# Relational layer with layer normalisation: first half in quarters, later turns and normalising, and the bias added to x by GpSimd

## What is computed

```python
# adj: (8, 1024, 1024) int32, x: (8, 1024, 128) float32
# relation ids are 1..4, weight: (4, 128, 128), bias: (128,)
masks = (adj[None] == rel_ids[:, None, None, None]).astype(x.dtype)
h = jnp.einsum('rbnm,bmd->rbnd', masks, x)
y = jnp.einsum('rbnd,rdo->bno', h, weight)
z = x + (y + bias)
out = (z - mean(z)) / sqrt(var(z) + 1e-5)      # over the last axis
```

## Time and profile before

| | us |
|---|---|
| median of 3 runs (126.42 to 127.32) | 127.29 |
| the profiled execution | 128.38 |
| its span | 126.6 |
| PE busy | 104.6 (83%) |
| DVE busy | 96.2 (76%) |
| ACT busy | 83.4 (66%) |
| POOL busy | 79.8 (63%) |

### The profile page before, as it was taken

The page is one execution under the profiler, slowest core; times in us unless marked ns, Lnnn a source line. Parts: engine busy times, 40 slices in busy tenths (PEclk is TensorE's granted clock), DMA queues, the critical chain, the costliest instruction groups (busy, mean ns, idle before and its releaser), DMA issues.

```text
span 126.6 us, 1876 instructions
## 1 busy us (share of the span) xinstructions
PE 104.6 (83%) x551; PEld 85.0 (67%) x559; DVE 96.2 (76%) x243; ACT 83.4 (66%) x114; POOL 79.8 (63%) x76
## 2 busy tenths in 40 slices
PE   5933399989999789899999999999999999997100
PEld 2312288687878567678887887788879886896000
DVE  0249925277949999999999999999999997639820
ACT  4056780766649178699589939994999499951400
POOL 6008000067253989899989989999999899043510
PEclk9996557999999999999999999999999999999855
DMA  4999999999999999999999999999999700400620
GB/s 116 409 422 430 425 422 432 422 430 405 434 419 419 427 417 425 410 436 417 422 365 409 425 422 359 421 427 427 388 281 418 311 18 0 166 0 0 250 87 8
DMA packets 7362, 42.15 MB, mean 333 GB/s; under 512 B 819, under 2 KB 1206, under 8 KB 3254
## 3 DMA queue, kind: packets, MB, share of 16 engines
q1 hardware_dynamic: 7350, 42.01, 81.7%
HBM read 37.82 MB, written 4.19 MB: 332 GB/s over the span
## 4 chain that ended last, share of the span: by engine, by line
DMA 25%; DVE 22%; PE 18%; ACT 11%; POOL 11%; issue 6%; SPq 2%; DVEq 0%; POOLq 0%; ACTq 0%
DMA adj_sb<-in_adj_dram 25%; PE h_ps L187 13%; POOL scale L217 10%; ACT maskT L355 9%; DVE mask L426 6%; DVE stats L205 4%; DVE var_eps L214 4%; DVE total L440 3%; PE tp_ps L178 2%; PE y_ps L199 2%; DVE mean_var L210 2%; DVE out_sb L221 2%; ACT out_sb L374 1%; ACT h_sb L362 1%; SPq L244 1%
## 5 line engine op out<-in xcount | busy, mean ns | idle before, releaser
L355 ACT ACTIVATE maskT<-tp_ps 128x2048 fp32r<-128x2048 fp8e5 x32 | 59.7, 1873 | 8.1 <-PE tp_ps L178 8.1
L426 DVE TENSOR_SCALAR mask<-adj_sb 128x2048 uint8<-128x2048 uint32 x32 | 39.7, 1266 | 16.2 <-DMA adj_sb<-in_adj_dram 16.1
L217 POOL TENSOR_TENSOR scale<-var_eps,power 128x4 f32<-128x4 f32 (+1 forms) x17 | 44.3, 2608 | 0.6 <-DVE var_eps L214 0.6
L187 PE MATMUL h_ps<-maskT,x_hi 128*128 128x512 f32 (+1 forms) x136 | 35.7, 406 | 1.1 <-ACT maskT L355 0.9
L187 PE MATMUL h_ps<-maskT,x_lo 128*128 128x512 f32 (+1 forms) x136 | 33.8, 391 | 0.0
L178 PEld LDWEIGHTS tp_ps<-identity,mask 128*128 128x128 f32 x128 | 20.3, 204 | 13.8 <-DVE mask L426 10.2
L187 PEld LDWEIGHTS h_ps<-maskT,x_hi 128*128 128x128 f32 x136 | 24.7, 197 | 6.6 <-ACT maskT L355 2.3
L178 PE MATMUL tp_ps<-identity,mask 128*128 128x128 f32 x128 | 22.3, 300 | 7.9 <-DVE mask L426 7.8
L374 ACT ACTIVATE out_sb<-total,shift,scale 128x128 f32<-128x128 f32 x31 | 13.7, 488 | 19.8 <-POOL shift L319 19.8
L187 PEld LDWEIGHTS h_ps<-maskT,x_lo 128*128 128x128 f32 x136 | 23.5, 189 | 3.9
L199 PE MATMUL y_ps<-w_sb,h_sb 128*128 128x128 f32 x128 | 17.3, 277 | 1.6 <-ACT h_sb L362 1.3
(11 more groups left out here) (32 smaller groups left out, 33.3 us busy)
## 6 DMA issues: line engine op xcount, KB each, us to landing
adj_sb<-in_adj_dram SPq DMA_DIRECT2D x32, 1024.0 KB, 12.2
x_sb<-in_x_dram SPq DMA_DIRECT2D x8, 512.0 KB, 5.9
out_dram<-out_sb SPq DMA_DIRECT2D x7, 512.0 KB, 16.5
out_dram<-out_sb SPq DMA_DIRECT2D x1, 256.0 KB, 2.4
out_dram<-out_sb SPq DMA_DIRECT2D x2, 128.0 KB, 1.9
w_sb<-in_L_gnn_weight_dram SPq DMA_DIRECT2D x1, 64.0 KB, 6.5
bias_rows<-in_L_gnn_bias_dram SPq DMA_DIRECT2D x3, 0.5 KB
```

Source lines behind the costliest of these rows:

```text
L187: last = nc.tensor.matmul(h_ps[:, bank, 0:n], (x_hi, x_lo)[part][:, slot, t, :], maskT[:, places, t // WORD, t % WORD, :], start=(first an ...
L217: nc.gpsimd.tensor_tensor(scale[:, slot, tiles], var_eps[:, slot, tiles], power[:, tiles], ALU.pow).then_inc(done, by)
L355: nc.scalar.activation(maskT[:, u % NMT], turned_codes(u % NTP), ACT.Copy, accum_out=counts[:, u:u + 1]).then_inc(expanded, 1)
L426: nc.vector.tensor_scalar(mask[:, u % NMASK], adj_sb[:, u % NADJ].bitcast(u32), CAP, SET, ALU.min, ALU.mult).then_inc(masked, 1)
```

## The change

It has five parts.

- **Bias.** The bias is loaded once, over all partitions, on ACT's queue, together with the weight. The bf16 split, its placing, and the spreading products on PE (one per half, two for the last) are gone. Instead POOL adds the bias to all of `x_sb` of a batch (`add_bias`), right behind the `lo` of that batch; DVE's `add` waits for it (`biased`). In the general path the same add stands too.
- **First half in quarters.** The products, the copy and the order of the first half go by units instead of by half. POOL, not ACT and DVE, makes the parts of batch 0. PE gets 8 and 4 products on a scratch tile in between (`keep_warm`).
- **Later turns.** In the loop PE issues the products with `x_hi` before the turn of the unit 2hf+3 instead of after it.
- **Later normalising on ACT.** ACT normalises half hf-3 in each round instead of half hf-2.
- **Check and last half.** The check for other relations is made before the last adds, and its product stands ahead of the last products. SP loads x of the next batch one place later in its order.

The core of the diff:

```diff
+        def add_bias(x_slot, done):
+            nc.gpsimd.tensor_tensor(x_sb[:, x_slot], x_sb[:, x_slot],
+                                    bias_rows[:, :].unsqueeze(1).to_broadcast([P, TILES, D]), ALU.add).then_inc(done, 1)
-        def spread_bias(y, tiles):
-            n = tiles.stop - tiles.start
-            nc.tensor.matmul(y[:, 0:n, :], spread[:, :], bias_parts[:, 0:n, :], start=True, stop=False)
...
@@ sync
-            load_unit(1)
-            sp.wait_ge(bias_cleared, 1)
-            for q in PARTS:
-                sp.dma_start(bias_rows[q:q + 1, :], bias.unsqueeze(0)).then_inc(bias_loaded, 16)
-            sp.dma_start(w_sb[:, 0, :], weight[0]).then_inc(weights_loaded, 16)
-            for u in range(2, UNITS):
+            for u in range(1, UNITS):
                 load_unit(u)
-                if u % CH == 1 and u // CH + 1 < B:
+                if u % CH == (2 if u >= CH else 3) and u // CH + 1 < B:
                     load_batch(u // CH + 1)
-                if u == 3:
-                    load_batch(1)
@@ gpsimd
+            def bias_in(b):
+                if b == 0:
+                    pool.wait_ge(bias_loaded, 16)
+                pool.wait_ge(lo_made, b + 1)
+                add_bias(b % NX, biased)
-            split_bias()
+            hi(0)
+            lo(0)
+            bias_in(0)
             for b in range(B):
                 if b + 1 < B:
                     hi(b + 1)
...
                 if b + 1 < B:
                     lo(b + 1)
+                    bias_in(b + 1)
                 scales_half(2 * b)
@@ scalar
+            copy_quarter(0, 0)
+            expand(2)
+            copy_quarter(0, 1)
+            expand(3)
+            for hf in range(1, HALVES - 1):
+                if hf >= 2:
                     copy_half(hf - 1)
                 expand(2 * hf + 2)
                 expand(2 * hf + 3)
-                if hf >= 2:
-                    finish_half(hf - 2)
+                if hf >= 3:
+                    finish_half(hf - 3)
             copy_half(HALVES - 2)
+            finish_half(HALVES - 4)
+            copy_quarter(HALVES - 1, 0)
             finish_half(HALVES - 3)
-            copy_quarter(HALVES - 1, 0)
             copy_quarter(HALVES - 1, 1)
@@ vector
             def add(b, y, tiles, count, by):
                 dve.wait_ge(projected, count)
+                dve.wait_ge(biased, b + 1)
...
+            find_others()
             add_half(HALVES - 2)
             measure_half(HALVES - 2)
             finish_half(HALVES - 3)
-            find_others()
@@ tensor
+            turn(0)
+            keep_warm(8)
+            hi_quarter(0, 0)
+            turn(1)
+            lo_quarter(0, 0)
+            turn(2)
+            hi_quarter(0, 1)
+            lo_quarter(0, 1)
+            turn(3)
...
+            for hf in range(2, HALVES - 1):
+                hi_products(hf)
                 if 2 * hf + 3 < UNITS:
                     turn(2 * hf + 3)
-                hi_products(hf)
-                if 2 * hf + 4 < UNITS:
-                    turn(2 * hf + 4)
-                if hf >= 1:
-                    project_half(hf - 1)
+                project_half(hf - 1)
                 lo_products(hf)
+                if 2 * hf + 4 < UNITS:
+                    turn(2 * hf + 4)
```

More of the change, by code:

```diff
@@ L131, in relational_layer @@
         g_split = sem("g_split")
+        g_biased = sem("g_biased")
         g_masked = sem("g_masked")
@@ L198, in project @@
                 for r in range(relations):
-                    last = nc.tensor.matmul(y[:, n, :], h_of(r)[:, s], w_sb[:, r, :], start=False,
-                                            stop=(r == relations - 1 and s == tiles.stop - 1))
+                    last = nc.tensor.matmul(y[:, n, :], h_of(r)[:, s], w_sb[:, r, :], start=(r == 0),
+                                            stop=(r == relations - 1))
             last.then_inc(done, by)
@@ L379, in finish_half @@
                 finish(hf // 2, range(HT * (hf % 2) + 1, HT * (hf % 2) + HT, O), 2 * (hf + 1), 2)
+            act.dma_start(bias_rows[:, :], bias.unsqueeze(0).to_broadcast([P, D])).then_inc(bias_loaded, 16)
+            act.dma_start(w_sb[:, 0, :], weight[0]).then_inc(weights_loaded, 16)
             expand(0)
-            act.wait_ge(topped, 1)
-            nc.scalar.activation(flat(x_hi[:, 0]), flat(x_top[:, :]).bitcast(fp32), ACT.Copy).then_inc(hi_made, 1)
             expand(1)
-            for hf in range(HALVES - 1):
-                if hf >= 1:
+            copy_quarter(0, 0)
[3 more added lines that the diff above has]
+            for hf in range(1, HALVES - 1):
+                if hf >= 2:
                     copy_half(hf - 1)
@@ L483, in find_others @@
                 nc.vector.tensor_scalar(above[:, 1:2], above[:, 0:1], FULL, None, ALU.is_gt).then_inc(flag_step, 1)
-            def place_bias():
-                dve.wait_ge(bias_split, 3)
-                for q, part in zip(PARTS, (bias_rows, bias_rest, bias_fine)):
-                    last = nc.vector.tensor_copy(bias_parts[q:q + 1], upper(part[q:q + 1, :]).unsqueeze(1).to_broadcast(
-                        [1, HT, D]))
-                last.then_inc(bias_split, 1)
             convert(0)
             top(0)
-            convert(1)
-            dve.wait_ge(topped, 1)
-            take_lo(nc.vector, 0, 0, lo_made)
-            convert(2)
-            place_bias()
-            convert(3)
+            for u in (1, 2, 3):
+                convert(u)
+            top(1)
             convert(4)
-            for hf in range(HALVES - 1):
-                for u in (2 * hf + 5, 2 * hf + 6):
+            convert(5)
+            for hf in range(1, HALVES - 1):
+                for u in (2 * hf + 4, 2 * hf + 5):
                     if u < UNITS:
@@ L514, in _ @@
             finish_half(HALVES - 3)
-            find_others()
+            dve.wait_ge(flag_counted, 1)
+            nc.vector.tensor_copy(flag[:, :], tp_ps[0:1, 0, 0:1]).then_inc(flag_ready, 1)
             add_quarter(0)
@@ L650, in _ @@
                     for half in range(2):
-                        spread_bias(y_ps[:, half], HALF[0])
                         project(lambda r: h_all[:, r], y_ps[:, half], R, HALF[half], g_projected, 1)
```

70 lines of the change are left out of this document (29 added, 41 removed).

## The result

| | before | after |
|---|---|---|
| median, us (lowest to highest) | 127.31 (126.42 to 127.34) | 133.71 (132.76 to 134.26) |
| profiled execution, its span | 128.38, 126.6 | 133.56, 131.8 |

The changed kernel takes 1.051 times as long, interval 1.044 to 1.059: +6.4 us, where 132.7 us in all was forecast.

What follows compares the result with a forecast made beforehand. POOL's closed chain, in mutual exclusion with DVE on SBUF, was taken as the bound. 8.4 - 0.7 - 1.9 - 0.4 = +5.4 us on 127.3 gave 132.7 us, range 126.5 to 138.5, chance 0.60.

Steps and rivals of the forecast that it cites:

- What bounds the kernel: Mid-kernel, POOL's SBUF work and DVE's conversions, tops, normalising and variance steps exclude each other; POOL's closed chain takes 12.0-12.3 us per batch.
- I take 2.4: POOL's bias add behind x_lo: each takes 2.4 us, like x_lo, bounded by 1.04 and 3.4; a batch grows by all of it.
- Four adds, the first partly covered. I take 3.5: Of eight POOL adds, those of batches 3 to 6 count; 3.5 x 2.4 = +8.4 us, bounds 3.1 and 17.
- That of batch 7 … 0: The last batch's add, behind the last x_lo where few conversions are left, costs 0.
- Where the wait lies: The add, right behind x_lo in POOL's chain, waits through DVE's normalising, conversions and top; a batch grows from 12.0 to 14.4 us.
- the exclusion passes on: Rival: the add starts right behind DVE's variance step and DVE's conversions wait; net 1.4 us a batch, 129.2 us; chance 0.13.
- The add is absorbed: Rival: the add only shortens waits in POOL's scales, beside DVE's free 2.2 us stretches; 124.3 us, or 123; chance 0.12.
- The clock falls: Rival: mid-kernel PE pauses of 2 to 3 us a batch drop its clock, adding 8 us: 141 us; chance 0.07.
- Spreading products, -0.7: PE: removing the bias products gains nothing mid-kernel, but 0.7 us behind the last conversion.
- Later normalising, -1.9: ACT: normalising one half later removes a 1.88 us wait for a shift near the end, -1.9 us; 0 in the middle.
- Start: 0 … all of this lies under the loads: At the start, quarters and bias and weight on ACT's queue gain 0, hidden by loads until 36.91 us; bounds -2 and +1.
- later turns … 0: In PE's loop, products come 0.4 us earlier and turns 2 us later, inside POOL's cover: 0, -1 to +1.

Runs made afterwards that it cites:

- the kernel of 121.04: Kernel before with PE's later turns, ACT's later normalising, and DVE's conversions one unit later in its order: 121.04 us, 0.950 of before.
- the best kernel: Changed kernel with the bias split and spread on PE as before instead of POOL's add, bias rows and weight on ACT's queue: 118.04 us, 0.925 of before.

## Why the forecast was right, and where it was not

The number was right because two errors cancel. In the runs the sum reads -8.2 (all but the add) +14.5 (the add) = +6.3; the prediction's reads -3.0 + 8.4 = +5.4.

- **What bounds the kernel.** Right: the exclusion of POOL and DVE. With half an add the wait is half as long, without it gone. That POOL's chain paces every batch is not shown: without the add PE, too, is busy for 9.4 to 10.00 of 10 us, so the three engines lie close together.
- **"I take 2.4".** Right, 2.45 in the trace. The Trainium skill ("GPSIMD Engine Reference", 3.1 Elementwise — side-by-side cycle accounting) has 4497 ns for an add of twice the length, an estimate of 2.25 for this one; the trace's 2.45 is near it.
- **"Four adds, the first partly covered. I take 3.5".** Wrong, and this is the mis-sized term: 8.4 predicted, 14.5 measured. Unlike what the step says, the adds from batch 2 to batch 6 all count. Conversions of unit 12 start 1.5 us apart in the two traces (46.9 and 45.4). From there to unit 28 four batches take 4 x 14.0 = 56.1 us with the add, and 46.3 without. 1.5 + 9.8 is the 11.4 by which the last conversion moves, to 0.1. Two things were missed. POOL's idles before 41 us were idles at other places than the add's, and could not take it. And per batch the add costs 14.0 less 11.2 or 12.0, since without it the chain also loosens: in the first two closed batches the variance steps take 0.65 us and not 1.44.
- **"That of batch 7 … 0".** Wrong: 2.3 us. It stands at 114.61, DVE's pair waits for it (the 2.68 at 114.47 above), and the whole tail stands behind that pair. With the 1.5 and 9.8 above that makes the 13.7 us by which the spans of the two traces differ.
- **Where the wait lies.** The prediction had the add behind normalising, conversions and top. It came right behind `x_lo`, between two normalising steps: the place of the rival *the exclusion passes on*, with about the forecast's size (2.0 to 2.8 us a batch, not the rival's 1.4). The Trainium skill's lock for one instruction ("SBUF — State Buffer", Who interferes with whom) describes this place well, but not the scales: the one issued at 66.40 again waited through two conversions. Neither reading alone fits both.
- ***The add is absorbed*.** False for this order, and yet the best pointer of the four: two places later, 9.0 of 14.5 us are absorbed (10.6 by the faster runs). It decides at DVE's free stretch, as written: in three of five batches the add ran beside add, statistics and aggregates, with `x_lo` in the other half's stretch, and DVE did not wait for either longer than 0.2 us.
- ***The clock falls*.** False: PE's pauses of 1.6 us left the granted clock at 1.00.
- **Spreading products, -0.7.** Not seen: without them the kernel is 1.2 us slower (119.26 against 118.04). That kernel also loads the bias as 128 rows, and its first conversion starts at 7.7 instead of 5.7. The two were not parted; in the changed kernel the late start was worth at most 0.8.
- **Later normalising, -1.9.** About 2.6, at the least 0.8, with the other parts there. In the profile after, ACT stands 4.5 us for the shift in all, but 27.6 for PE's turns.
- **Check, -0.4.** No experiment has it alone.
- **"Start: 0 … all of this lies under the loads" and "later turns … 0".** This is the other step that failed. The later turns are worth 6.7 us when the rest is there, and nothing with the later normalising alone; the later conversions 4.1 and 5.5. Turns, normalising and conversions together give 6.3 (127.38 to 121.04). The step looked at whether work fits under the loads. It did not look at which work stands *behind a load's wait* in DVE's strict order, nor at the projection, which DVE's add waits for, behind PE's turns. The prediction named "a gain at the start or the end" as what it might have missed. It was both: the kernel without the add has its last conversion 3.1 us earlier than the kernel before (98.4 for 101.5), where the prediction had 0, and takes 5.4 less from there to the end (19.7 for 25.1), where it had 3.0.

From 121.04 to 118.04, three more us come with the quarters, the check and the order of the start and the end. They were not tried singly. The granted clock may be part of it: from 12 to 18 us it is 0.50 in the kernel of 121.04 and 1.00 in the best one, which has the quarters and `keep_warm` there.

## What to carry to other kernels

Where two engines exclude each other, an instruction costs by its place in the order as much as by its length: 14.5 us in one place and 4 to 5.5 us in another, for the same eight adds. In a program run strictly in order, ask of each wait for a load what stands behind it that already could run; taking one such wait out of the way was worth 4 to 5.5 us at equal work. A forecast whose sum is right proves none of its terms: run the main term alone and undone (+12.1, -14.5), and the rest alone (-9.4).

## What the runs showed of the hardware

- A wait behind the exclusion need not cover the whole instruction. In the changed kernel the scale issued at 75.03 ends at 77.32, 0.05 us after the second conversion (77.27), where 0.87 was seen before, and the shift behind such a scale takes 0.49 instead of 0.20 (63.40). The likeliest reading is that its reading fitted in between DVE's steps and only its writing waited; that is argued, not shown.
- One program can fall into two patterns: in the best kernel the variance step takes 0.70, 0.65, 0.66 us in the first batches of the closed chain, and 1.47 later, with batches of 11.2 and 12.0 us. The kernel with the add placed later scatters by 4.7 us from run to run, the others by 0.5 to 2.4. What tips it stays open.
- Small loads on a second queue can slow the big loads beside them. The changed kernel's ACT queue (q10) carries bias and weight, 0.13 MB in 288 packets, and the windows before its first conversion move 280, 227 and 226 GB/s against 393, 401 and 414 before:

```profile
3.00:4.00 1.00, 1.00 (x4) 0.39 (x3) 0.00 (x0) 0.01 (x1) 0.00 (x0) 1.00 0.83 280
4.00:5.00 1.00, 1.00 (x6) 0.46 (x5) 0.00 (x0) 0.00 (x0) 0.00 (x0) 1.00 0.72 227
5.00:6.00 1.00, 0.48 (x3) 0.00 (x0) 0.00 (x0) 0.00 (x0) 0.00 (x0) 1.00 0.87 226
```

The first conversion is 1.96 us late by it (7.64 for 5.68), but at the end it is worth at most 0.8. The second queue alone does not do it. The best kernel has the same weight and three rows of bias on ACT's queue, 150 packets, moves 426, 397 and 398 GB/s in these windows, and starts to convert at 5.69. It lacks the bias over 128 rows, and its weight is issued at 3.11 us, where the changed kernel issues its bias at 0.8. Which of the two matters was not tried.
